# Cross attention in a decoder on one Trainium2 core: both late score units first, output projections between the key folds, two fold copies on VectorE

## The reference, cut to what matters

```python
qh = (q @ Wq).reshape(B, N, 16, 64).transpose(0, 2, 1, 3)
kh = (kv @ Wk).reshape(B, M, 16, 64).transpose(0, 2, 1, 3)
vh = (kv @ Wv).reshape(B, M, 16, 64).transpose(0, 2, 1, 3)
scores = jnp.einsum('bhnd,bhmd->bhnm', qh, kh) * 64 ** -0.5
attn = jax.nn.softmax(scores, axis=-1)
out = jnp.einsum('bhnm,bhmd->bhnd', attn, vh)
return out.transpose(0, 2, 1, 3).reshape(B, N, 1024) @ Wo + bo
...
x = _layernorm(x + _L0_attn_ref(x, ...), axis=-1)
x = _layernorm(x + _L0_xattn_ref(x, ctx_512, ...), axis=-1)
```

## Time and profile before

| | us |
|---|---|
| median of 3 runs | 2625.72 (2625.55 to 2626.34) |
| the profiled execution | 2626.34 |
| its span, from first to last instruction | 2624.2 |
| TensorE busy in the span | 2351.5 (90%) |
| VectorE busy | 1606.1 (61%) |
| ScalarE busy | 1108.6 (42%) |
| GpSimd busy | 875.9 (33%) |

### The profile page before, as it was taken

How to read it: one execution, slowest core, us unless ns; L and a number is a source line. 1 busy time by engine, 2 the same in 40 slices (tenths; PEclk the granted TensorE clock), 3 DMA queues, 4 the chain that set the end, 5 groups by cost and what they waited for, 6 DMA issues and landing times. The chain is left out here.

```text
span 2624.2 us, 55940 instructions
## 1 busy us (share of the span) xinstructions
PE 2351.5 (90%) x20985; PEld 1614.2 (62%) x21080; DVE 1606.1 (61%) x3416; ACT 1108.6 (42%) x2397; POOL 875.9 (33%) x1231
## 2 busy tenths in 40 slices
PE   8988999999999997979899899899989699939996
PEld 6765666666666664555555566555556599826664
DVE  1237777777777775746566666656656499862221
ACT  2333343333333332246656666666666244402221
POOL 1111110111111010026555655655654355522342
PEclk9999999999999998989999999999999799959998
DMA  5100000000000001200000000000000012131330
GB/s 161 43 0 2 1 0 0 0 0 0 0 0 0 0 0 32 89 27 0 0 0 0 0 0 0 0 0 0 0 0 1 1 64 96 64 110 49 111 113 30
DMA packets 52743, 65.20 MB, mean 25 GB/s; under 512 B 5969, under 2 KB 45606, under 8 KB 52696
## 3 DMA queue, kind: packets, MB, share of 16 engines
q1 hardware_dynamic: 49624, 56.47, 6.7%
q0 software_dynamic: 3072, 8.07, 1.0%
HBM read 43.88 MB, written 20.97 MB: 25 GB/s over the span
## 5 line engine op out<-in xcount | busy, mean ns | idle before, releaser
L369 PE MATMUL B_ps_s<-B_xk,B_xT 128*32 128x308 f32 x4096 | 284.9, 424 | 12.8 <-ACT B_xk L504 12.8
L390 PE MATMUL B_ps_m<-B_wo,B_oT 128*128 128x256 f32 x1024 | 239.6, 388 | 2.1 <-ACT B_oT L523 2.1
L1513 DVE TENSOR_TENSOR D_att<-D_ps_s,D_dexp 128x1024 f32<-128x1024 f32 x128 | 154.5, 1207 | 131.5 <-ACT D_dexp L1331 124.6
L1083 POOL TENSOR_SCALAR_AFFINE_SELECT D_att<-D_att 128x1024 f32<-128x1024 f32 x128 | 139.9, 1093 | 260.5 <-DVE D_att L1513 260.5
L390 PEld LDWEIGHTS B_ps_m<-B_wo,B_oT 128*128 128x128 f32 x1024 | 190.6, 191 | 52.2 <-ACT B_oT L523 18.1
L491 ACT ACTIVATE B_prob<-B_prob 128x616 f32<-128x616 f32 x128 | 92.9, 726 | 300.4 <-DVE B_prob L602 300.4
L369 PEld LDWEIGHTS B_ps_s<-B_xk,B_xT 128*32 128x32 f32 x4096 | 124.6, 109 | 148.4 <-issue 26.1
L600 DVE TENSOR_REDUCE B_mx<-B_ps_s 128x8 f32<-128x616 f32 x128 | 101.0, 789 | 150.9 <-PE B_ps_s L369 150.9
L285 POOL TENSOR_TENSOR B_veps<-B_mv,eps 128x2 f32<-128x2 f32 x32 | 6.2, 195 | 537.0 <-DVE B_mv L584 537.0
L1091 POOL TENSOR_TENSOR D_orms<-D_oms,D_half 128x32 f32<-128x32 f32 x32 | 174.1, 5439 | 2.7
L1182 PE MATMUL D_ps_s<-D_q2T,D_kT 32*128 32x256 f32 x1024 | 147.8, 404 | 6.8 <-DVE D_att L1513 3.6
(11 more groups left out here) (297 smaller groups left out, 5274.9 us busy)
## 6 DMA issues: line engine op xcount, KB each, us to landing
res<-in_x SPq DMA_DIRECT2D x16, 512.0 KB, 3.4
x_d<-res SPq DMA_DIRECT2D x8, 1024.0 KB, 4.5
out<-E_fin SPq DMA_DIRECT2D x8, 1024.0 KB, 7.1
wi<-in_L_ffn_wi SPq DMA_DIRECT2D x8, 1024.0 KB, 5.0
wo<-in_L_ffn_wo SPq DMA_DIRECT2D x8, 1024.0 KB, 7.5
C_wgu<-in_L_ffn_gate_up SPq DMA_DIRECT2D x8, 512.0 KB, 3.6
C_wdn<-in_L_ffn_down_proj SPq DMA_DIRECT2D x8, 256.0 KB, 2.7
B_wqT<-in_L_xattn_WqT SPq DMA_DIRECT2D x1, 1024.0 KB, 11.6
```

The lines of the kernel that those rows point to most:

```text
L369: last = nc.tensor.matmul(ps_s[u % 2][q * G:(q + 1) * G, g, 0:HQ * S], xT[:, par, k, (2 * u + g) * G:(2 * u + g + 1) * G], xk[:, par, k].r ...
L390: last = nc.tensor.matmul(ps_m[:, bank, 0:D], oT[:, m, t * P:(t + 1) * P], wo[:, m], start=m == 0, stop=m == MT - 1)
L1083: nc.gpsimd.affine_select(out=att[:, n % 2], in_=att[:, n % 2], compare_op=ALU.is_ge, fill=0.0, base=0, pattern=[[0, HT], [1, P]], channel ...
L1513: nc.vector.tensor_tensor(att[:, n % 2].rearrange("p h i -> p (h i)"), ps_s[:].rearrange("p a n -> p (a n)"), dexp[:, n % 2], ALU.mult).th ...
```

## The change

On TensorE, an even batch now makes score units 2 and 3 one after the other, then both output projections, and puts the values' projection behind the key projections. An odd batch makes both score units, then fold 0, output projection 0, fold 1, output projection 1, fold 2, and after these the transposes and the values' projection; fold 0 waits for the copies of the attention output. On ScalarE the order follows: the fold copies 0, 1 and 2 stand ahead of the exponentials 2 and 3 and of the copy of x, and the values' copy stands behind the key copies. For folds 4 and 5 ScalarE copies one bank only; VectorE copies the other (`copy_folded` of its own, semaphore `xk_ready2`), between the last normalisation of an odd batch and the maxima of the next. VectorE's loop goes over pairs of batches.

```diff
+        xk_ready2 = sem("xk_ready2")
...
                 scores(2, 0)
-                if prev:
-                    project_out(b - 1, 0, 0)
                 pe.wait_ge(sub_ready, b * U + 2)
                 scores(3, 0)
                 if prev:
+                    project_out(b - 1, 0, 0)
                     project_out(b - 1, 1, 1)
                 transpose_x(nb, 2)
                 if more:
                     pe.wait_ge(ctxk_ready, j + 2)
                     project_k(0, 3)
-                project_values(nb, 0, 1, (lambda: pe.wait_ge(res_ready, b * 2 - 1)) if prev else nothing,
-                               (lambda: pe.wait_ge(res_ready, b * 2)) if prev else nothing)
-                pe.wait_ge(xT_ready, nb + 1)
-                if more:
+                    pe.wait_ge(xT_ready, nb + 1)
                     project_k(1, 2)
                     pe.wait_ge(k_ready, j * 3 + 4)
                     project_k(2, 3)
+                else:
+                    pe.wait_ge(xT_ready, nb + 1)
+                project_values(nb, 0, 1, (lambda: pe.wait_ge(res_ready, b * 2 - 1)) if prev else nothing,
+                               (lambda: pe.wait_ge(res_ready, b * 2)) if prev else nothing)
...
                 scores(2, 1)
-                project_out(b - 1, 0, 0)
                 pe.wait_ge(sub_ready, b * U + 2)
                 scores(3, 1)
                 if more:
+                    pe.wait_ge(oT_ready, b * 2)
                     fold_keys(0, (2, 3))
-                project_out(b - 1, 1, 1)
+                project_out(b - 1, 0, 0)
                 if more:
                     pe.wait_ge(xk_ready, j * NA + 7)
                     fold_keys(1, (2, 3))
+                project_out(b - 1, 1, 1)
+                if more:
+                    pe.wait_ge(xk_ready, j * NA + 8)
+                    fold_keys(2, (2, 3))
                     pe.wait_ge(res_ready, b * 2 - 1)
                     transpose_x(nb, 0)
-                    pe.wait_ge(xk_ready, j * NA + 8)
-                    fold_keys(2, (2, 3))
...
                     pe.wait_ge(xk_ready, j * NA + 12)
+                    pe.wait_ge(xk_ready2, j * 2 + 4)
                     scores(0, 0)
...
+            pe.wait_ge(xk_ready2, 1)
             project_values(0, 0, 1, lambda: pe.wait_ge(xk_ready, NA - 1), nothing)
             pe.wait_ge(xk_ready, NA)
+            pe.wait_ge(xk_ready2, 2)
             scores(0, 0)
...
                 act.wait_ge(xk_done, j * NA + (n + 1))
-                for c in range(2):
+                for c in range(2 if n < NA - 2 else 1):
...
                     copy_k(j + 1, 0, 3)
-                copy_v(nb, 1, 0, 1)
-                if more:
                     copy_k(j + 1, 1, 2)
                     copy_k(j + 1, 2, 3)
+                copy_v(nb, 1, 0, 1)
...
                 exponential(b, 1)
+                if more:
+                    copy_folded(j + 1, 0, (2, 3))
                 exponential(b, 2)
                 if more:
-                    copy_folded(j + 1, 0, (2, 3))
+                    copy_folded(j + 1, 1, (2, 3))
                 exponential(b, 3)
                 if more:
-                    copy_folded(j + 1, 1, (2, 3))
+                    copy_folded(j + 1, 2, (2, 3))
                     copy_x(nb, 0, 0)
-                    copy_folded(j + 1, 2, (2, 3))
...
-            def body(b, first=False, more=True):
+            def copy_folded(j, n, bank):
+                k, g = STEPS[n]
+                ms = GROUPS[g]
+                dve.wait_ge(xk_done, j * NA + (n + 1))
+                nc.vector.tensor_copy(xk[:, :, k].rearrange("p b (m c) s -> p c m b s", c=2)[:, 1, ms[0]:ms[-1] + 1],
+                                      ps_m[:, bank, 0:len(ms) * 2 * S].rearrange("p (m b s) -> p m b s", b=2, s=S)).then_inc(xk_ready2, 1)
+
+            def body(b, j=None, first=False, more=True):
...
                 normalise(b, 3, first)
+                if j is not None:
+                    copy_folded(j + 1, 4, 1)
+                    copy_folded(j + 1, 5, 3)
...
+            copy_folded(0, 4, 1)
+            copy_folded(0, 5, 3)
             shift(0, 0)
             shift(0, 1)
             body(0, first=True)
-            with dve.Fori(1, B - 1) as b:
-                body(b)
+            body(1, 0)
+            with dve.Fori(1, B // 2 - 1) as j:
+                body(j * 2)
+                body(j * 2 + 1, j)
+            body(B - 2)
             body(B - 1, more=False)
```

## The result

The changed kernel takes 2587.52 us (median of 4 runs, 2586.63 to 2588.03) where the kernel before took 2625.64 beside it: a ratio of 0.9855, 95% interval 0.9838 to 0.9872, 38 us faster. The forecast was 2589, within 2581 to 2606.

The account below looks back on a forecast made before the run. TensorE bounds the stage, with 2.80 us of holes a pair. Gains of 1.35 + 0.81 + 0.28 = 2.44 us a pair, 34.2 over 14 pairs, with batches 1, 31 and first folds 36.5, gave 2589 us, within 2581 to 2606.

Parts of the forecast that it names:

- Even batch: TensorE, even batches: key projections fill the 1.15 us hole before the values' projection; with 0.20 for joined runs, 1.35 us.
- the joints: TensorE, even batch: joining both score units and both output projections saves 0.2 us, with bounds of 0 and 0.35.
- the cover named: Even batch: keys end only 0.13 us after the residual sum could be there, so any delay of it is paid in full.
- Odd batch: Odd batches: the new order gains 0.81 us up to the fourth fold, and the fold copies 0.28.
- The wait of 0.1 inside the values' projection: TensorE, odd batch: the last third waits a new 0.1 us for ScalarE's copy of x, there at 15.75.
- The fold copies: Odd batch end: VectorE takes half of folds 4 and 5, so scores start after 3.52 us, not 3.80; gain 0.28 (0 to 0.33).
- Batch 1: Batch 1, outside the loop of pairs: has the odd batch's gain, 1.1 us.
- batch 31: Last batch: scores first removes VectorE's 1.00 us wait for the fourth score unit; all behind it ends 1.0 us earlier.
- The first folds: Folds ahead of batch 0: same six copies with partly hidden ends, put at 0.2 us.
- Joints worth nothing: Rival: joined runs save nothing and the last third waits 0.25 us instead of 0.1; 2594 us, chance 0.14.
- VectorE's chain: Rival: VectorE's residual sum comes d later, costing 2d a pair; 2603 to 2626 us, chances 0.09 (part left) and 0.05 (none).
- ScalarE's queue: Rival: odd batch's exponential of unit 2, behind fold 0's copies, delays the residual sum; slower, 2631 us, chance 0.04.

Follow-up runs that it names:

- run 4: Changed kernel with score units and output projections of the even batch alternating again, keys still ahead of the values' projection: 2591.46 us, ratio 0.9870.
- run 10: Changed kernel plus an unused VectorE reduction over 768 columns ahead of the two residual additions in each batch: 2610.55 us, ratio 0.9945.
- run 11: Changed kernel with ScalarE's exponentials 2 and 3 of the odd batch ahead of the fold copies as before: 2587.87 us, ratio 0.9859.
- run 8: Changed kernel with VectorE also making the second copy of fold 3: 2581.88 us, ratio 0.9830.
- run 6: Changed kernel plus an unused VectorE reduction of 256 columns behind the last normalisation of each batch: 2586.07 us, ratio 0.9848.
- run 9: The changed kernel itself again, as base for the last three runs: 2588.01 us, ratio 0.9855.
- run 7: Changed kernel with the last third of the odd batch's values' projection moved behind fold 5, ScalarE copying it last: 2579.77 us, ratio 0.9826.
- run 1: Kernel before with only the even batch's new order on TensorE and ScalarE: 2601.09 us, ratio 0.9905.
- run 12: Changed kernel with the values' last third behind fold 5, fold 3's second copy on VectorE, and VectorE's last transposes behind its copies: 2578.44 us, ratio 0.9823.
- run 2: Kernel before with only the odd batch's new order on TensorE and ScalarE, all fold copies on ScalarE: 2615.94 us, ratio 0.9961.
- run 3: Kernel before with only VectorE's second copies of folds 4 and 5 and its loop over pairs: 2620.82 us, ratio 0.9981.
- run 5: Changed kernel plus an unused VectorE reduction of 256 columns ahead of the two residual additions in each batch: 2592.10 us, ratio 0.9873.

## Why the prediction was right

It was right in its steps, and 1.5 us off in its sum (2587.5 for 2589). That the sum is so near is partly luck, for in it errors of both signs cancel: 14 even batches gave 4.8 us more than forecast, 14 odd ones 1.5 less, and batch 30, on which nothing was put, lost 1.55.

- *Even batch, 1.35 us forecast, 1.69 measured.* The keys filled the hole as described: the values' projection starts at 14.12 (797.47 less 783.35; 14.18 before, 14.3 forecast) and the scores follow at 15.44 (near 15.7 forecast). The mis-sized term is the joints: 0.2 forecast, 0.31 by run 4. Two more were not in the sum: the scores start 1.32 us after the values' projection, where the key projections of the kernel before started 1.43 after it, and the sixteen key products in one run take 2.39 us (795.08 to 797.47), where the kernel before made six in 0.95 and ten in 1.51. Together that is 0.29 of the 0.34. That VectorE's additions would now be met to the tenth was the cover named; run 10 shows it.
- *Odd batch, 1.09 forecast, 0.98 measured.* The fourth fold starts at 16.30 (16.23 forecast). The transposes take 0.59 to the next work where the even batch's 0.44 was used; the odd batch's own row gave 0.63 (854.05 to 854.68). The wait of 0.1 inside the values' projection does not show in TensorE's products: the copy of x ends at 15.63 (820.86 + 0.60 less 805.83; 15.75 forecast), and the last third came later by the longer transposes. Only its weight loads waited for the copy, 0.23 us (the row at 821.52 above). The fold copies gain 0.24 where 0.28 was forecast: 3.56 to the scores for 3.52. The copies are as long as read off, and the scores start 0.07 after VectorE's second (825.14 + 0.48 to 825.69), for which 0.08 was put; but that copy starts 0.05 after fold 5's end, which was counted as nothing.
- *Outside the loop.* Batch 1 gained 0.99 (1.1 forecast). From the first scores of batch 31 to its attention values it is 15.20 us for 16.27, 1.07 (1.0 forecast). The first folds gained 0.23 (0.2).
- *Not counted.* Batch 30 became 1.55 us longer, 24.07 for 22.52; the last section says how.
- *The rivals.* Joints worth nothing: refuted by run 4. VectorE's chain: right as a price (run 10), and at the edge, but nothing in the change moved it. ScalarE's queue: exponential 2 started at 7.25 (813.08 less 805.83), as it had at 7.26, behind copies that ended at 6.4 (811.21 + 1.01); run 11 undoes this order and changes nothing.

The Trainium skill's figures for copies out of PSUM (page VectorE: DVE Perf Modes, section on the TRN2 errata) give an estimate of 0.61 and 0.45 us for VectorE's two halves; the trace has 0.64 and 0.48, so the measurement decides. That a half is dearer on VectorE than on ScalarE is so (0.48 for 0.43 at 308 columns), and did not matter: what counts is that two engines copy at once.

The stage as a whole, from the first fold to the end of the last projection out, fell from 849.9 us to 812.0. The rows that bound it, of the kernel before and of the changed one:

```profile
176.86 1.85 PE L346 MATMUL B_ps_m<-B_kT,B_wqT 64*128 64x154 f32 x24 [0.78 <-ACT B_xT L511]
...
1017.90 8.86 PE L390 MATMUL B_ps_m<-B_wo,B_oT 128*128 128x256 f32 x32 [2.11 <-ACT B_oT L523]
```

```profile
175.18 1.85 PE L347 MATMUL B_ps_m<-B_kT,B_wqT 64*128 64x154 f32 x24 [0.78 <-ACT B_xT L517]
...
978.35 8.86 PE L391 MATMUL B_ps_m<-B_wo,B_oT 128*128 128x256 f32 x32 [2.09 <-ACT B_oT L529]
```

The difference is 37.9 us, and the terms above account for it. The 14 pairs give 37.25 (2.66 each on the average), batch 0 gives 0.13, and 37.25 + 0.13 + 0.99 + 1.07 + 0.23 - 1.55 = 38.1, less 0.27 for the last attention values, which took 5.42 for 5.15.

## What to carry to other kernels

Where the fullest engine has short holes, look for work of its own that stands behind the hole and doesn't need what the hole waits for, and price it by the hole. Then write down how much later the awaited result may come: here it was 0.0 us in the even batch and 0.07 in the odd, so the next gain in that place has to come from the other engine's chain, and work for that engine must stand behind the result. Run the parts alone: here the three add up to within 0.01 us a pair, and the new place of the exponentials within one of them was worth nothing.

## What the runs showed of the hardware

**Behind a hole of 2.2 us the clock fell in some traces and not in others.** In batch 30 the hole ahead of the values' projection grew from 1.93 to 2.22 us, because TensorE came to it earlier. Behind it TensorE ran at its lower level. Busy time by engine and granted clock (PEclk) in the changed kernel:

```profile
943.40:945.60 2.20, 0.06 (x1) 0.00 (x0) 2.17 (x5) 0.60 (x1) 0.10 (x1) 0.99 0.00 0
945.60:948.20 2.60, 2.52 (x24) 1.34 (x28) 2.50 (x6) 0.53 (x1) 0.00 (x0) 0.50 0.03 6
```

A granted clock of 0.50 is 1.2 GHz. The same 24 products took 2.79 us in this trace, 1.50 in run 8:

```profile
945.68 2.79 PE L353 MATMUL B_ps_m<-B_wv,B_ctx_v 128*32 128x256 f32 x24 [2.22 <-DVE res L630]
```

```profile
943.36 1.50 PE L353 MATMUL B_ps_m<-B_wv,B_ctx_v 128*32 128x256 f32 x24 [2.22 <-DVE res L633]
```

The hole is the same 2.22 us in both. It was followed by the lower level in the changed kernel and in runs 6, 9 and 11, in run 7 (2.23 us) a little later (the 64 score products took 6.00 for 4.36), and not in runs 1, 8 and 12. The 1.93 us of the kernel before and of runs 2, 3 and 4 were not followed by it, nor were the 2.54 of run 5; the 3.07 of run 10 were. So the length of the hole alone does not decide. The fall costs about 1.6 us once: batch 30 takes 24.07 us with it, 22.47 in runs 1, 8 and 12. What decides was not tried, and that the hole is the cause is not shown.
